# Decoder layer on one Trainium2 core: the next batch's input work placed earlier in the order tables, x2 normalized by ScalarE, the mixer residual summed by TensorE through the identity

## What is computed

```
def _layernorm(x): (x - mean) / sqrt(var + 1e-5)

x = _layernorm(x + mamba(x))            # mamba(x) returns x + out, so the sum is 2x + out
x = _layernorm(x + slots(x, ctx))
x = _layernorm(x + ffn(x))

mamba:  xn = layer_norm(x)*g + b;  u, z = split(xn @ W_in.T)
        u = silu(conv4(u) + conv_b);  dt_in, B, C = split(u @ W_x.T)
        dt = softplus(dt_in @ W_dt.T + dt_bias)
        h[t] = exp(dt*A) * h[t-1] + dt*B*u;   y = sum_n h*C + u*D
        out = (y * silu(z)) @ W_out.T
slots:  three rounds of: rmsnorm, scores against the context, softmax over the slots,
        renormalized weights, update, GRU cell
ffn:    h = relu(x @ W_fc.T)**2;  y = h @ W_proj.T;  spikes of five steps on y, summed / 5
```

## Time and profile before

| | us |
|---|---|
| median of 3 runs | 1699.95 |
| lowest, highest | 1696.39, 1705.75 |
| the profiled execution | 1699.65 |
| its span, first to last instruction | 1697.8 |
| start of pass 0 (first dt matmul) | 41.6 |
| start of passes 6, 7 (first DVE row behind the meeting) | 1148.7, 1339.9 |
| start of the drain part (first ACT row) | 1530.7 |

### The profile page before, as it was taken

The page is one execution under the profiler, slowest core; times in us unless marked ns, Lnnn a source line. Parts: engine busy times, 40 slices in busy tenths (PEclk is TensorE's granted clock), DMA queues, the critical chain, the costliest instruction groups (busy, mean ns, idle before and its releaser), DMA issues. The chain is left out here.

```text
span 1697.8 us, 16460 instructions
## 1 busy us (share of the span) xinstructions
PE 1360.2 (80%) x5536; PEld 808.5 (48%) x5536; DVE 1310.5 (77%) x1508; ACT 989.2 (58%) x1547; POOL 866.1 (51%) x432
## 2 busy tenths in 40 slices
PE   4465787787888789887888789887888789887787
PEld 1244444454445445454445455454445455453354
DVE  2899688876887898968987888968987888973335
ACT  3644575537665576737765567737765567734522
POOL 0566257644666266644766267644766267640100
PEclk9775898797999899997999989997999989999898
DMA  4733343306332443306332343306331343300000
GB/s 165 262 134 114 140 148 112 111 25 226 123 105 70 140 161 104 118 15 225 128 115 66 128 159 111 119 17 225 126 115 68 125 162 111 116 19 2 12 0 25
DMA packets 64875, 188.96 MB, mean 111 GB/s; under 512 B 6304, under 2 KB 22560, under 8 KB 64832
## 3 DMA queue, kind: packets, MB, share of 16 engines
q1 hardware_dynamic: 64832, 188.43, 32.1%
HBM read 183.62 MB, written 4.78 MB: 111 GB/s over the span
## 5 line engine op out<-in xcount | busy, mean ns | idle before, releaser
L492 POOL TENSOR_TENSOR reg_a<-reg_a,cb 128x1024 f32<-128x1024 f32 (+1 forms) x256 | 600.5, 2355 | 308.3 <-DVE reg_a L1393 302.8
L1393 DVE TENSOR_TENSOR_SCAN reg_a<-reg_a,pb 128x1024 f32<-128x1024 f32 x256 | 584.8, 2284 | 27.3 <-ACT reg_a L1129 15.5
L1129 ACT ACTIVATE reg_a<-dt,neg_a 128x511 f32<-128x511 f32 x512 | 334.6, 710 | 54.1 <-DVE reg_a L1393 53.6
L769 PE MATMUL py<-ident,reg_a 128*128 128x128 f32 x1984 | 286.7, 296 | 83.3 <-POOL reg_a L492 83.3
L1384 DVE TENSOR_TENSOR pb<-bb,pb 128x1024 f32<-128x1024 f32 x256 | 314.5, 1228 | 24.4 <-DVE reg_a L1393 2.9
L769 PEld LDWEIGHTS py<-ident,reg_a 128*128 128x128 f32 x1984 | 250.3, 153 | 172.7 <-POOL reg_a L492 113.8
L630 PE MATMUL px<-hT,whh 128*128 128x512 f32 x252 | 120.2, 604 | 0.0
L457 POOL TENSOR_TENSOR xs<-xs,hT 128x1024 f32<-128x1024 f32 x24 | 56.5, 2354 | 111.5 <-ACT xs L1049 111.5
L734 PE MATMUL pc<-x2T,w_fc 128*128 128x512 f32 x192 | 99.4, 643 | 8.2 <-ACT reg_m L1056 8.2
L742 PE MATMUL pc<-w_pr,reg_m 128*128 128x256 f32 x384 | 90.9, 382 | 8.6 <-ACT reg_m L1058 8.6
L742 PEld LDWEIGHTS pc<-w_pr,reg_m 128*128 128x128 f32 x384 | 69.6, 190 | 25.7 <-ACT reg_m L1056 13.4
(11 more groups left out here) (255 smaller groups left out, 2337.1 us busy)
## 6 DMA issues: line engine op xcount, KB each, us to landing
bb<-bc_rows SPq DMA_DIRECT2D x256, 512.0 KB, 3.6
cb<-bc_rows SPq DMA_DIRECT2D x64, 512.0 KB, 6.3
xin<-x_in SPq DMA_DIRECT2D x9, 512.0 KB, 3.3
xs<-x_in SPq DMA_DIRECT2D x8, 512.0 KB, 3.3
x_out<-reg_m SPq DMA_DIRECT2D x5, 512.0 KB, 3.4
w_in<-w_inT_in SPq DMA_DIRECT2D x1, 1024.0 KB, 6.8
w_fc<-w_fcT_in SPq DMA_DIRECT2D x1, 1024.0 KB, 10.9
w_pr<-w_prT_in SPq DMA_DIRECT2D x1, 1024.0 KB, 13.1
```

What stands on the lines that cost most here:

```text
L492: pool.tensor_tensor(h[:, g % HR, 0:n], h[:, g % HR, 0:n], cb[:, 2 * q:2 * q + n], ALU.mult).then_inc(s["hc_done"], 1)
L769: mm = pe.matmul(py[:, cols_], h[:, g % HR, j, cols_], ident[:], is_transpose=True, start=(q == 0 and j == 0 and i2 == 0), stop=(q == PAIR ...
L1129: ins = act.activation(d_a[:, g % DR, j, 1:], dt[:, c, 1:], ACT.Exp, scale=neg_a[:, c * NS + n + j:c * NS + n + j + 1])
L1393: dve.tensor_tensor_scan(h2[:, g % HR], d_a2[:, g % DR], pb[:, 1:3, :].rearrange("p a t -> p (a t)"), 0.0, ALU.mult, ALU.add).then_inc(s[" ...
```

## The change

The change touches the order tables and the steps that they name.

- Start: `cols` and `w_in` get semaphores of their own, so that ACT, DVE and PE no longer wait for all first weights; PE runs 36 multiplications of the identity into an unused bank ahead of the first transposes; the first transposes wait for one token block each; the function tables of ACT (SILU, then LN_EXP) are loaded ahead of their use, LN_EXP now at the end of a pass in `keep_bc` and no longer at its start.
- The next batch's norm and transposes stand at slots 10, ("mid", 11), 18 and 20. In slot 20 ACT copies them before it reads up 1 1, and PE's norm 2 waits for the copies.
- u 0 and u 1 go into banks pb3 and pc ahead of `final` 0 in slot 30, u 2 and u 3 into px in slot 32; `conv` is cut into its taps; u 3 gathers in `uth`; `xp` is cut into four parts into bank py, laid between outp 2 and outp 3 and behind it.
- `final` 0 on DVE stands at slot 33, behind scan 31. `final` 1 on DVE is only the shift (128 x 4), and ACT applies it at the end, four times 128 x 256.
- `outr` on PE (slot 32) adds xres into the four quarters with the identity; DVE's four additions go, and its statistics and x1 read PSUM. y_back of the last chunk comes behind outp 1.
- `sp_ln` stands ahead of `weigh` 0 on ACT, `spike` 5 behind scan 0, `zed` 3 at ("mid", 9), up 0 x of ACT one slot later, POOL's keep 2 at slot 27, the second round's gate_x 0 ahead of down 0 1 and the third round's gate_h 2 in slot 25.

```diff
+SILU = "silu_and_others"
+TURN = 1
-        u_banks = (px[:, 0, :], px[:, 1, :], pb[:, 3, :], px[:, 0, :])
+        u_banks = (pb[:, 3, :], pc[:], px[:, 0, :], px[:, 1, :])
+        def u_acc(c):
+            return u2[:, c] if c < DT - 1 else uth[:, 0]
+        op_banks = pb[:, 1:3, :].rearrange("p a (b e) -> p (a b) e", e=E)
-        loads = [(cols, cols_d), (w_in, k_rows(w_inT)), (w_x, k_rows(w_xT)), (w_dt, w_dtT)]
+        loads = [(w_x, k_rows(w_xT)), (w_dt, w_dtT)]
+        WARM = 36
...
-                      (28, ("cand_x", 2, 0), ("down", 1, 3)), (29, ("cand_x", 2, 1), ("turn",)),
-                      (30, ("final", 0), ("u", 0), ("u", 1)), (32, ("outp", 0)), (34, ("outp", 1), ("u", 2)),
-                      ("end", ("u", 3), ("outp", 2), ("outp", 3), ("xp",)))
+                      (28, ("cand_x", 2, 0), ("down", 1, 3)), (29, ("cand_x", 2, 1)), (30, ("u", 0), ("u", 1), ("final", 0)),
+                      (32, ("u", 2), ("u", 3), ("outp", 0), ("outr",)), (33, ("outp", 1)), (34, ("outp", 2), ("xp", 0), ("xp", 1)),
+                      ("end", ("outp", 3), ("xp", 2), ("xp", 3)))
...
-                      (("mid", 26), ("next_shift",)), (("mid", 28), ("hold", 2)), (28, ("down", 1, 3)), (30, ("final", 0)), (("mid", 32), ("conv", 0)),
-                      ("end", ("final", 1), ("conv", 2)))
+                      (("mid", 32), ("conv", 0, 0)), (32, ("conv", 0, 1)), (("mid", 33), ("conv", 0, 2)),
+                      (33, ("final", 0), ("conv", 2, 0), ("conv", 2, 1), ("conv", 2, 2)), ("end", ("final", 1)))
...
             pe.wait_ge(consts_done, 6)
-            next_transposes()
+            for _ in range(WARM):
+                pe.matmul(pb[:, 0, 0:P], ident[:], ident[:], start=True, stop=True)
+            for i2 in range(TT):
+                pe.wait_ge(s["next_norm"], i2 + 1)
...
+                    if mamba and k == TURN + 1:
+                        pe.wait_ge(s["xnT_ready"], ET)
                     pe.wait_ge(s["sq_ready"], k + 1)
...
+                elif step == "outr":
+                    pe.wait_ge(s["xres_load"], 16)
+                    for i2 in range(TT):
+                        pe.matmul(op_bank(i2), ident[:], xres[:, i2], start=False, stop=False, skip_group_check=True)
                 elif step == "xp":
-                    x_proj()
+                    if k == 0:
+                        pe.wait_ge(s["half_kept"], 2)
+                    x_proj(k)
...
                         if chunk_end(g) == DT - 1:
-                            if ffn:
-                                pe.wait_ge(s["unit_read"], reads_before_slot(g))
+                            pe.wait_ge(s["conv_step"], 2 * (KC - 1))
...
-                act.activation(xp, px[:, 1, :], ACT.Copy).then_inc(s["bc_kept"], 1)
+                act.activation(xp, py[:], ACT.Copy).then_inc(s["bc_kept"], 1)
+                act.preload_act_table_set(LN_EXP)
...
+                elif step == "final" and k == 1:
+                    shifted("x2", x2, x2)
...
                     if k == 1:
-                        norm_apply("x2", x2, x2)
+                        norm_shift("x2")
...
                 if mamba:
-                    dve.wait_ge(s["xres_load"], 16)
-                    for i2 in range(TT):
-                        dve.wait_ge(s["op_full"], 2 * (i2 // 2) + 2)
-                        dve.tensor_tensor(xres[:, i2], xres[:, i2], op_bank(i2), ALU.add).then_inc(s["res_done"], 1)
-                    norm_stats("post", xres, eps=LN_EPS / 4)
+                    norm_stats("post", op_banks, eps=LN_EPS / 4)
                 filler("post")
                 if mamba:
-                    norm_apply("post", xres, x1)
+                    norm_apply("post", op_banks, x1)
```

## The result

| | before | after |
|---|---|---|
| median, us | 1700.09 | 1672.79 |
| lowest, highest | 1696.39, 1705.75 | 1670.28, 1675.76 |
| profiled execution, its span | 1699.65, 1697.8 | 1672.55, 1670.6 |

The ratio is 0.9827, with a 95% interval from 0.9802 to 0.9852: 27 us faster, where 36 had been forecast. The time lies in the forecast range, 9 us above its centre. Two of the three terms of the sum came out close (the start 9.5 us for 9.1, the tail 4.4 a pass on average for 4.7), the third didn't. Ratios and their intervals here leave out executions over 1.5% slower than the same kernel's fastest, which is two in all, both of the kernel with the norm late.

The account below looks back on a forecast made before the run. DVE and PE were taken to share the bound, neither full, with the last scan 6.9 us late. 1699.65 - 9.1 (start) - 7 x (4.7 tail - 0.85 middle) = 1663.6, forecast 1664, range 1646 to 1688.

Parts of the forecast that it names:

- Bound and tail: End of passes 1 to 7: PE's queue is the path; x1 25.3 us behind hT, gaining 4.7 a pass.
- The PSUM source: DVE's statistics and norm at the pass end, reading PSUM: rows taken to show no price, so the sum has none.
- Start: Before the first pass: earlier norm and transposes bring the first xp copy to 30.6 instead of 40.2; taken as -9.1 us.
- Inside the passes: Passes 1 to 7, up to the end of the third round: four moves sum to +0.85 us a pass.
- Term (b): Next input's statistics, 2.0 us, free in slot 23 but not in slot 10; slot 14's wait takes over half: +0.7.
- Term (c): Slot 20: ACT's two copies (1.45 us) stand ahead of up 1 1 and round 2's norm: +0.8.
- Term (d): Slots 25 to 29: PE's transposes and ACT's norm gone where DVE waits for PE; transposes' part given back, -0.95.
- Term (a): Pass start: table load of 1.28 us goes, sp_ln (1.67) stands ahead of weigh 0; net +0.3 for round 0.
- The middle takes its full price: Inside the passes: Term (b) counts on both sides, nothing given back, +3.5 a pass, 1682; 0.18 together with the last rival.
- The slower rival: PE's tail queue at clock 0.71 takes 22.0 us instead of 15.6: +2.55 a pass, 1708 in all; chance 0.10.
- The last rival: Tail: four steps ahead of PE's sum each late by own wait, gaining only 2.5 us: 1679; 0.18 with the full-price rival.

Follow-up runs that it names:

- the kernel with the norm late: Changed kernel with the next input's statistics, shift, norm and transposes back in slots 23, mid 26, 26 and 29: 1665.6 us, ratio 0.9772.
- the last kernel: Changed kernel with sp_ln behind weigh 0, next input's statistics between recol 1 and renorm 1 (slot 14), shift ahead of hold 1: 1649.6 us, ratio 0.9715.

## Why the prediction was right, and where it was off

**Bound and tail: right.** PE's queue behind hT was forecast at 5.7 + 15.6 us, and 25.3 with the norm (its terms add up to 25.2); it is 25.3. The late scan of DVE has no price: taken away alone it gives nothing. That the figure agrees to the tenth is luck: inside this sum two errors of opposite sign cancel. PE's queue ends 0.6 us sooner than forecast (at 20.7 behind hT instead of 21.3), and what follows takes 4.6 instead of 3.9. The gain is 4.7 us in passes 3 to 7, but 4.3 and 3.2 in passes 1 and 2, 31.0 in all where 32.9 had been forecast.

**The PSUM source: the step was wrong.** The prediction saw no price in the rows and gave the sum none; the rows were of other instructions. The statistics go from 411 to 423 ns, and L1436 is an addition, but the norm, a `tensor_scalar`, goes from 408 to 539 ns, 131 more, 0.52 us a pass:

```profile
L1286 DVE TENSOR_SCALAR x<-pb,post_mv,post_rstd 128x256 f32<-128x256 f32 x32 | 15.2, 539 | 9.0 <-POOL post_rstd L461 9.0
```

The Trainium skill has this in "VectorE: DVE Perf Modes", section "The perf-mode tier table" with its part "Why PSUM operands drop a tier": an f32 `tensor_scalar` takes two elements a cycle from SBUF and one from PSUM. For 256 elements at the page's 0.96 GHz that is 133 ns, an estimate from its figures, and the trace agrees. The fixed cost of the same page of the Trainium skill, which the prediction cites, would give 65 ns for each kind of instruction (an estimate from its figures), and the statistics' 12 ns don't agree with it.

**Start: the number right in the compared pair** (9.5 against 9.1), of which 5.0 come with the earlier norm and the warming, and 4.5, by difference, with u 3's own bank and `xp` in quarters. Over all traces it is 5 to 10 us, since both starts move by some 2 us. The working has slips. Its terms add up to 30.2 and not 30.6, and 40.2 less 30.6 is 9.6, for which no reason is given why 9.1 was taken. The copy ended at 30.30 because two errors cancel: the warming products end at 11.4 instead of 14.5, and what follows them takes 18.9 us instead of 15.7, since ACT gets to u 2 and u 3 only at 22.27, behind its first silu, and the last half of `xp` takes 2.50 us.

**Inside the passes: the mechanism half right, the sizes wrong.** Term (b) was taken as +0.7, "the other wait takes more than half of it". The step cost 3.1 between scans 10 and 12 (3.4 in pass 4), 2.0 for the statistics and 1.1 for the shift, for which the term had nothing. Behind it slot 14 took back 1.1 to 1.3 in passes 2 to 4; in passes 5 to 7, at the lower clock, it cost another 0.6. In the last kernel 1.8 of the 2.0 that the statistics no longer cost came back as a wait, so up to scan 15 they had been nearly free; the shift had not. Term (c), +0.8, measured 0.6 between scans 19 and 23 in most passes, where DVE's wait for a decay grew from 0.8 to 1.4 as in the rows above. Term (d), -0.95, measured -0.6 in passes 3 to 7. Term (a), +0.3, hid two things: in passes 3 to 7 scan 0 comes 1.5 to 1.6 us earlier without the table load, and round 0 loses 1.1 of it up to scan 4 in passes 6 and 7, and all of it or more in passes 3 to 5 (up to 2.2). Two terms were missing: from pass 2 on hold 1 in slot 18 costs 1.2 to 1.3 us more (in pass 5 it waits 2.1 us for PE and not 0.8), with the norm early or late, so that the new order of PE in slots 15 and 16 is the likely cause, which no run undid; and the clock at the z projection, -2.0 to -3.0 between scans 4 and 5 in passes 3 to 7, +1.0 and +0.4 in passes 1 and 2. That last one was luck: it covered up the price of (b) and is why the sum in the loop (1.4) looks near its forecast (0.85). Over all seven passes the middle cost 14.9 us where the sum had 6.0; these 8.9 us are the step that failed, and what else was off (tail, start, pass 0, the meetings between passes, drain) cancels to 0.1.

**The rivals.** "The middle takes its full price" had 3.5 a pass; passes 1 and 2 did about that, +5.0 and +2.7. The slower rival looked for the lower clock in the tail's queue. There it didn't come (1.00 from 1104 to 1128). A lower clock does cost this kernel time, though, 1.4 to 3.0 us a pass where it falls on the z projection, in the next pass. The last rival, four steps laid ahead of the last sum over states and each late by its own wait, did not come true either: PE has no gap there.

## What to carry to other kernels

An instruction moved off a place where its engine waits has its full price at once wherever the engine doesn't. A later wait may take the price back, as it did with the statistics, or the next engine may wait too, and TensorE's clock may fall behind that, as in four of twelve passes here. So after a reorder follow one instruction per slot through the pass, before and after, and beside it the granted clock; the sum of a pass hides gains and losses of 3 us that cancel. And price a new operand place by rows of the same operation: that an addition costs the same from PSUM says nothing of a `tensor_scalar`.

## What the runs showed of the hardware

**A DVE instruction with two SBUF inputs waits for the POOL instruction that is running.** In all eight passes after, the shift of the next input starts while POOL multiplies, and ends with it: here 1382.35 + 1.34 = 1383.69, and POOL:

```profile
1381.30 2.37 POOL L507 TENSOR_TENSOR reg_a<-reg_a,cb 128x1024 f32<-128x1024 f32 x1
```

1381.30 + 2.37 = 1383.67. The ends lie within 0.03 us of each other in all eight (1.30 to 1.36 us), and in a ninth case in pass 1 of the last kernel (1.13 us). With POOL idle the same instruction takes 0.13 to 0.17. It is not every instruction that waits: the scans, with one input in PSUM, take 2.29 us beside POOL and 2.28 without it, and the statistics of the next input, with one input, 0.41 either way. The last product by C on DVE (reg_a and cb, both in SBUF) is of the same kind: 692 ns on average before, 2.24 us in the rows of the tail above, and 2.22 in the kernel whose scan 31 alone was moved, since both bring it beside POOL's products. In the tail it starts at 1106.35 within a product of POOL that ends at 1108.04, and ends 0.55 behind that; POOL's last, half as wide, then takes 1.73 us. All of it is off the path there. The Trainium skill states it in "SBUF — State Buffer", section "Who interferes with whom": a DVE instruction with two SBUF inputs contends with a GpSimd instruction that reads SBUF, and whichever starts first holds the port to its end. The trace agrees. Read beside POOL's rows for the place that the shift was moved to, it would have pointed to the 1.2 us that term (b) left out.

**The same instructions take two times.** In the last kernel passes 4 and 5 take 183.1 us up to x1 and passes 6 and 7 186.7, with the same instructions and data sizes. Scan 23 comes 3.5 us later in the latter. Half of it, 1.7 us, arises between scans 22 and 23, where the granted clock from 115 to 120 us is 0.72, and 1.00 in the former; 0.9 to 1.0 stand already at scan 4, and 0.9 come in slot 14. What tips a pass from one into the other I can't say from these runs.
